# Latent attention core: seeding the score banks of two key tiles with four products on quarters of the array

## The chip, the cores and the metric

The kernel runs on one core of a Trainium2 chip. The metric is the device time of one execution in microseconds (us), as a median over the runs. The engines that matter here are PE (TensorE: matrix products; its weight loads are listed apart as PEld), ACT (ScalarE), DVE (VectorE), POOL (GpSimd) and SP (SyncE, which here only issues transfers).

## The reference, cut to what matters

The program is a decoder of twelve stages over 2048 rows of width 256. One of them is attention of 512 queries per batch over 1536 keys (1024 context rows and the 512 rows themselves), 4 batches, 16 heads of depth 64:

```
q = lat @ Wq
kv_input = jnp.concatenate([x, lat], axis=1)
kv = kv_input @ Wkv
k, v = jnp.split(kv, 2, axis=-1)
dots = jnp.einsum('bhid,bhjd->bhij', q, k) * scale
attn = jax.nn.softmax(dots, axis=-1)
out = jnp.einsum('bhij,bhjd->bhid', attn, v)
```

The softmax subtracts the maximum of every query's row, so the maxima have to be known before the exponentials are taken.

## The kernel before, in words

`latent_core_stage` does this stage's scores, softmax and weighting. It works in 32 groups (4 batches of 8 groups), each a pair of heads; head 0 of the pair lies on rows 0 to 63 of the array and of every operand, head 1 on rows 64 to 127 (`strip(j)`). A group has `nkt` = 12 key tiles of 128 keys. Every product over the depth of 64 therefore comes as two instructions, one per head, on the upper and on the lower half of the array's rows.

Two passes overlap. **Pass A** (`pass_a`, line 1059) forms the scores of a later group in bf16, 128 queries by 512 keys at a time, twelve steps a group; DVE takes the maximum of each (`maxima`, line 1183). After the twelfth, PE turns the maxima (`turn`, line 1066), DVE negates them and splits them in two bf16 parts (`negate`, lines 1192 to 1195, semaphore `row_made`), and SP copies them by DMA into two rows per head of `max_row` (`row`, line 1025, semaphore `row_in`): row 0 and 1 of each half. **Pass B** forms the scores again in f32 with keys on the partitions. `scores(b, g, i)` first writes minus the maxima into the bank of each head with a bf16 product of ones by `max_row` (line 1077, the seed), then adds the f32 product of keys by queries on top (line 1079, two instructions per head). ACT takes the exponential of both banks in one instruction (line 1162, semaphore `exp_done`); POOL and DVE add the weights up (lines 1253 and 1202); `weigh` (line 1089) multiplies the weights by the values, with the two heads side by side in the array's columns; `spread` (line 1099) sums the totals over the keys once a group. The score banks are four: tile `i` uses two of them and tile `i + 1` the other two.

The order is written out by hand. For each pair of tiles PE does: scores of tile i, scores of tile i + 1, a pass A step, (in the fifth pair of a group) the turn, weighing of the two tiles before, (in the second pair) the spread, and a pass A step. Every engine runs the same loop: groups 0 and 1 are written out, a hardware loop of three turns holds groups 2 to 9, 10 to 17 and 18 to 25, and groups 26 to 31 are written out again. The row of maxima of group g + 1 is issued by SP within group g, as soon as `row_made` says so, and PE asks for it (`row_in`) just before the first seed of group g + 1.

```
for i in range(0, nkt, 2):
    scores(b, g, i)
    scores(b, g, i + 1)
```

Of the kernel before, what the change touches and what calls it, by code (L numbers as in the profile page):

```python
# [31 lines left out]
P = 128  # L32
# [6 lines left out]
QUAD = 32  # L39
# [879 lines left out]
def latent_core_stage(k, q_store, k_store, values, nk, scale, att_of):  # L919
# [4 lines left out]
    nc = k.nc  # L924
    HEADS, D, nq = 2, 64, S
    GROUPS = H // HEADS
    nqt, nkt, nwide = nq // P, nk // P, nk // BANK
# [3 lines left out]
    RING, V_RING, TILES = 4, 2, 6  # L931
    A0, B0, ACC, SIDE = 0, 2, 6, 7
    QUARTERS = 4
    QUARTER = nq // QUARTERS
    ROW_PARTS = 2
    assert NP == nkt and nkt % TILES == 0 and nkt % 2 == 0

    def strip(j):
        return slice(j * D, (j + 1) * D)
# [6 lines left out]
    with ExitStack() as held:  # L946
        def sb(what, shape, dt=F32):
            return held.enter_context(nc.sbuf_tensor(f"lc_{what}", shape, dt))

        q_tile = [sb(f"q{r}", [P, nq]) for r in range(RING)]  # L950
        k_tile = [sb(f"k{r}", [P, nk]) for r in range(RING)]
        v_tile = [sb(f"v{r}", [P, nkt, P]) for r in range(V_RING)]
        q_round, k_round = sb("q_round", [P, 2, nq], BF16), sb("k_round", [P, 2, nk], BF16)
        max_row, ones_row = sb("max_row", [P, 2, nq], BF16), sb("ones_row", [P, P], BF16)
# [4 lines left out]
        negative, max_parts = sb("negative", [SLOTS, P]), sb("max_parts", [SLOTS, ROW_PARTS, P], BF16)  # L959
# [8 lines left out]
        def at(b, g, per_group, n):  # L968
            return b * (GROUPS * per_group) + (g * per_group + n)

        def later(b, g, ahead):
            return b + (g + ahead) // GROUPS, (g + ahead) % GROUPS
# [4 lines left out]
        def exists(b, g):  # L977
            return number(b, g) is None or 0 <= number(b, g) < B * GROUPS

        def before(b, g, n):  # L980

            return number(b, g) is not None and number(b, g) < n
# [11 lines left out]
        def pair_at(b, g, i):  # L994

            p = i + AHEAD
            return (*later(b, g, 1 + p // NP), p % NP)

        def loads_done(b, g):
            return 32 * (b * (GROUPS // RING) + g // RING + 1)  # L1000
# [4 lines left out]
        @block.sync  # L1005
        def _(sync):
            k.clear_last_set(sync)

            def load_group(b, g):
                rows = slice(g * P, (g + 1) * P)  # L1010
                sync.dma_start(q_tile[g % RING][:], q_store[rows, bass.ds(b * nq, nq)]).then_inc(loaded[g % RING], 16)
                sync.dma_start(k_tile[g % RING][:], k_store[rows, bass.ds(b * nk, nk)]).then_inc(loaded[g % RING], 16)

            def load_values(b, g):
                sync.dma_start(v_tile[g % V_RING][:], values[bass.ds(b * nkt, nkt), :, g * P:(g + 1) * P].rearrange("i p c -> p i c")
                               ).then_inc(v_loaded[g % V_RING], 16)

            def row(b, g):

                if before(b, g, 1):  # L1020
                    sync.wait_ge(set_up, 1)
                sync.wait_ge(row_made, at(b, g, 1, 1))
                for j in range(HEADS):
                    for p in range(ROW_PARTS):
                        sync.dma_start(max_row[j * D + p:j * D + p + 1, g % 2, :].rearrange("o (i t) -> o i t", t=P),
                                       max_parts[j * nqt:(j + 1) * nqt, p, :]).then_inc(row_in, 16)

            load_group(0, 0)
            load_group(0, 1)
            load_values(0, 0)  # L1030
            load_group(0, 2)
            load_values(0, 1)
            row(0, 0)

            def group(b, g):

                if not before(b, g, 1):
                    sync.wait_ge(pv_done, at(b, g, nkt, 0))
                    if exists(*later(b, g, 1)):
                        load_values(*later(b, g, 1))  # L1040
                if exists(*later(b, g, 3)):
                    load_group(*later(b, g, 3))
                if exists(*later(b, g, 1)):
                    row(*later(b, g, 1))

            for_groups(sync, group)

        @block.tensor
        def _(pe):
# [15 lines left out]
                    pe.wait_ge(inverted, at(b, g, QUARTERS, -QUARTERS))  # L1065
                nc.tensor.transpose(k.ps[0:SLOTS, SIDE, 0:P], row_max[:, g % 2, :], k.ident[:, :]).then_inc(turned, 1)

            def scores(b, g, i):

                if i == 0:  # L1070
                    pe.wait_ge(loaded[g % RING], loads_done(b, g))
                    pe.wait_ge(row_in, 16 * HEADS * ROW_PARTS * at(b, g, 1, 1))
                if not (before(b, g, 1) and i < 2):
                    pe.wait_ge(exp_done, at(b, g, nkt, i - 1))
                out = [k.ps[:, B0 + (i % 2) * HEADS + j, 0:nq] for j in range(HEADS)]
                for j in range(HEADS):
                    nc.tensor.matmul(out[j], ones_row[strip(j), :], max_row[strip(j), g % 2, :], start=True, stop=False)
                for j in range(HEADS):
                    mm = nc.tensor.matmul(out[j], k_tile[g % RING][strip(j), i * P:(i + 1) * P], q_tile[g % RING][strip(j), :], start=False, stop=True)  # L1079
                mm.then_inc(s_ready, 1)  # L1080

            def weigh(b, g, i):
# [27 lines left out]
            def group(b, g):  # L1110
                last, following = later(b, g, -1), later(b, g, 1)
                for i in range(0, nkt, 2):
                    scores(b, g, i)
                    scores(b, g, i + 1)
                    beside_values, beside_scores = pair_at(b, g, i), pair_at(b, g, i + 1)
                    if exists(*beside_values[:2]):
                        pass_a(*beside_values)
                    if i == nkt - AHEAD and exists(*following):
                        turn(*following)
                    if i:  # L1120
                        weigh(b, g, i - 2)
                        weigh(b, g, i - 1)
                    elif exists(*last):
                        weigh(*last, nkt - 2)
                        weigh(*last, nkt - 1)
                    if i == 2 and exists(*last):
                        spread(*last, at(b, g, 1, 1))
                    if exists(*beside_scores[:2]):
                        pass_a(*beside_scores)
# [43 lines left out]
        def _(dve):  # L1173
# [14 lines left out]
            def negate(b, g):  # L1188
                dve.wait_ge(turned, at(b, g, 1, 1))
                if not before(b, g, 1):  # L1190
                    dve.wait_ge(row_in, 16 * HEADS * ROW_PARTS * at(b, g, 1, 0))
                nc.vector.tensor_scalar(max_parts[:, 0, :], k.ps[0:SLOTS, SIDE, 0:P], -1.0, None, ALU.mult).then_inc(high_made, 1)
                nc.vector.tensor_scalar(negative[:, :], k.ps[0:SLOTS, SIDE, 0:P], -1.0, None, ALU.mult).then_inc(high_made, 1)
                dve.wait_ge(high_made, at(b, g, 2, 2))
                nc.vector.tensor_tensor(max_parts[:, 1, :], negative[:, :], max_parts[:, 0, :], ALU.subtract).then_inc(row_made, 1)
# [1591 lines left out]
class ContextFeed:  # L2787
# [5 lines left out]
    RING = 4  # L2793
# [218 lines left out]
```

## Time and profile before

| | us |
|---|---|
| median of 3 runs | 5061.21 |
| fastest and slowest of them | 5048.93 and 5066.54 |
| the profiled execution's own time | 5067.82 |
| its span in the trace | 5066.0 |
| mean granted clock of TensorE | 0.89 |

The span is the time from the first to the last instruction of the profiled execution; 1.8 us lie outside it. The latent core takes some 960 us of it, from about 2842 to 3805 us. Times in the rows below are us from the span's start.

### The profile page before, as it was taken

How to read it: one execution, taken by the hardware profiler on the slowest of the kernel's cores; microseconds unless marked ns; L12 is line 12 of the kernel's file. 1: busy time of each engine (PE TensorE's matmuls, PEld its weight loads, DVE VectorE, ACT ScalarE, POOL GpSimd, SP SyncE). 2: the span in 40 equal slices, each digit the busy share in tenths (PEclk: the TensorE clock that was granted, in tenths of full speed). 3: DMA queues.
4: the chain of work that ended last, by engine and by line, in shares of the span. 5: the costliest groups of instructions: out<-in, count | busy, mean ns of one | idle time of the engine just before them, and what ended most of it. 6: DMA issues, size and time to landing. Idle time of an engine off the chain costs nothing. (4 is left out here: it accounts for less than half of the span.)

```text
span 5066.0 us, 69777 instructions
## 1 busy us (share of the span) xinstructions
PE 4205.1 (83%) x20328; PEld 1984.3 (39%) x20328; DVE 2850.2 (56%) x6426; ACT 2373.5 (47%) x4593; POOL 1482.9 (29%) x1306
## 2 busy tenths in 40 slices
PE   8669766689678997897979799999997988189986
PEld 5322355377443322573234233333335644012223
DVE  3448474501566884104860378778763265298866
ACT  4336431243233775233753355545551255269992
POOL 3111132212130111112120188778880223200111
PEclk9669987799887998898989899999998999579998
DMA  7555212354033332574324321221201044623421
GB/s 250 128 104 116 50 52 34 113 201 150 31 126 56 66 66 64 226 240 136 73 62 158 112 74 59 64 69 59 73 28 45 32 116 83 191 63 89 93 54 37
DMA packets 374291, 486.70 MB, mean 96 GB/s; under 512 B 84772, under 2 KB 288020, under 8 KB 360516
## 3 DMA queue, kind: packets, MB, share of 16 engines
q1 hardware_dynamic: 366528, 447.77, 31.8%
q0 software_dynamic: 6384, 32.61, 2.1%
q8 instruction: 137, 2.24, 0.2%
q10 hardware_dynamic: 1068, 2.66, 0.2%
q14 instruction: 174, 1.43, 0.1%
HBM read 325.07 MB, written 143.92 MB: 93 GB/s over the span
## 5 line engine op out<-in xcount | busy, mean ns | idle before, releaser
L1253 POOL TENSOR_TENSOR lc_totals<-lc_totals,lc_weights 128x1024 f32<-128x1024 f32 (+1 forms) x320 | 623.3, 1948 | 165.0 <-DVE lc_totals L1202 134.4
L1162 ACT ACTIVATE lc_weights<-ps 128x1024 f32<-128x1024 f32 x384 | 393.6, 1025 | 441.3 <-PE ps L1079 431.0
L1183 DVE TENSOR_REDUCE lc_part_max<-ps 128x2 f32<-128x1024 f32 x384 | 466.3, 1214 | 200.2 <-PE ps L1059 198.8
L1079 PE MATMUL ps<-lc_q,lc_k 64*128 64x512 f32 x1536 | 397.0, 595 | 0.0
L1089 PE MATMUL ps<-lc_weights,lc_v 128*64 128x512 f32 x1536 | 372.0, 605 | 0.0
L775 DVE TENSOR_REDUCE l1x_core_part_max<-ps 128x1 f32<-128x512 f32 x512 | 316.5, 681 | 74.8 <-PE ps L599 74.7
L771 DVE CUSTOM_DVE_ANT_0 l3x_core_unused<-ps,l3x_core_mask_q 128x512 f32<-128x512 f32 x512 | 330.8, 686 | 6.7 <-DVE l3x_core_row_max L779 4.9
L734 ACT ACTIVATE l3x_core_weights<-ps 128x512 f32<-128x512 f32 x512 | 327.2, 693 | 8.2 <-PE ps L667 7.9
L734 ACT ACTIVATE l1x_core_weights<-ps 128x512 f32<-128x512 f32 x512 | 266.0, 602 | 83.9 <-PE ps L667 83.8
L717 ACT ACTIVATE ps<-l3x_core_mask_k 128x512 f32<-128x512 f32 x384 | 270.2, 704 | 33.4 <-DMA l3x_core_mask_k<-in_mask_k 33.4
L599 PE MATMUL ps<-l3x_core_k,l3x_core_q 96*128 96x512 bf16 x512 | 215.4, 421 | 53.5 <-DVE l3x_core_part_max L771 38.5
L237 POOL TENSOR_TENSOR proj_parts<-proj_rest,proj_parts 128x512 bf16<-128x512 f32 x112 | 143.5, 1288 | 308.5 <-ACT proj_parts L174 308.2
L599 PE MATMUL ps<-l1x_core_k,l1x_core_q 96*128 96x512 bf16 x512 | 208.9, 411 | 17.2 <-DMA l1x_core_k<-k_parts 13.3
L667 PE MATMUL ps<-l3x_core_q,l3x_core_k 99*128 99x512 bf16 x512 | 199.9, 397 | 18.6 <-ACT ps L717 17.2
L667 PE MATMUL ps<-l1x_core_q,l1x_core_k 99*128 99x512 bf16 x512 | 191.6, 384 | 5.3 <-ACT l1x_core_weights L734 5.3
L1379 DVE SCALAR_TENSOR_TENSOR rn_z<-ps,rn_z 128x256 f32<-128x256 f32 x112 | 45.7, 416 | 261.2 <-PE ps L1350 192.2
L775 DVE TENSOR_REDUCE pyr_core_row_max<-ps 128x1 f32<-128x512 f32 x256 | 158.7, 680 | 54.7 <-PE ps L599 54.5
L1079 PEld LDWEIGHTS ps<-lc_q,lc_k 64*128 64x128 f32 x1536 | 148.3, 189 | 94.0 <-issue 64.9
L775 DVE TENSOR_REDUCE l2a_core_row_max<-ps 128x1 f32<-128x512 f32 x256 | 158.3, 680 | 37.1 <-PE ps L599 37.0
L1059 PE MATMUL ps<-lc_k_round,lc_q_round 64*128 64x512 bf16 x768 | 151.6, 391 | 32.7 <-DVE lc_part_max L1183 21.2
L1089 PEld LDWEIGHTS ps<-lc_weights,lc_v 128*64 128x64 f32 x1536 | 93.3, 136 | 210.3 <-issue 118.8
L734 ACT ACTIVATE pyr_core_weights<-ps 128x512 f32<-128x512 f32 x256 | 134.0, 602 | 79.3 <-PE ps L667 78.9
(479 smaller groups left out, 8594.9 us busy)
## 6 DMA issues: line engine op xcount, KB each, us to landing
cf_w<-in_L1f_w SPq DMA_DIRECT2D x32, 1024.0 KB, 7.3
lc_k<-latent_k SPq DMA_DIRECT2D x32, 768.0 KB, 6.6
lc_v<-latent_values SPq DMA_DIRECT2D x32, 768.0 KB, 4.9
k_parts<-proj_parts SPq DMA_DIRECT2D x56, 384.0 KB, 2.8
latent_k<-feed_staged SPq DMA_DIRECT2D x64, 256.0 KB
latent_values<-feed_staged SPq DMA_DIRECT2D x64, 256.0 KB
q_parts<-proj_parts SPq DMA_DIRECT2D x40, 384.0 KB, 2.9
q_parts<-proj_parts SPq DMA_DIRECT2D x40, 256.0 KB, 3.0
```

What stands on the lines that cost most here:

```text
L599: mm = nc.tensor.matmul(out, q_stack[r][0:rows_a, j, qs], k_stack[r][0:rows_a, j, keys], start=True, stop=not causal)
L667: mm = nc.tensor.matmul(out, k_stack[r][0:rows_b, j, ks], q_stack[r][0:rows_b, j, qs], start=not seeded, stop=not (causal or seeded), skip ...
L717: nc.scalar.activation(k.ps[:, B0 + (g * NS + s) % B_BANKS, 0:nq], seed, ACT.Copy).then_inc(filled, 1)
L734: nc.scalar.activation(weights[:, (g * NS + s) % WEIGHTS, qs], k.ps[:, B0 + (g * NS + s) % B_BANKS, qs], ACT.Exp, scale=scale).then_inc(ex ...
L771: nc.vector.tensor_tensor_reduce(unused[:, n % 2, :], scores, mask_q[:, qi, keys], 1.0, -3.0e38, ALU.add, ALU.max, out).then_inc(a_taken, 1)
L775: nc.vector.reduce_max(out, scores, AX).then_inc(a_taken, 1)
L1059: mm = nc.tensor.matmul(k.ps[:, A0 + j, :], q_round[strip(j), g % 2, qs], k_round[strip(j), g % 2, keys], start=True, stop=True)
L1079: mm = nc.tensor.matmul(out[j], k_tile[g % RING][strip(j), i * P:(i + 1) * P], q_tile[g % RING][strip(j), :], start=False, stop=True)
L1089: mm = nc.tensor.matmul(k.ps[strip(j), ACC, 0:nq], v_tile[g % V_RING][:, i, strip(j)], weights[:, i % TILES, j, :], start=i == 0, stop=i = ...
L1162: nc.scalar.activation(weights[:, i % TILES, :, :], k.ps[:, B0 + (i % 2) * HEADS:B0 + (i % 2 + 1) * HEADS, 0:nq], ACT.Exp, scale=scale).th ...
L1183: nc.vector.reduce_max(own, k.ps[:, A0:A0 + HEADS, :], AX).then_inc(a_taken, 1)
L1253: nc.gpsimd.tensor_tensor(total, total, own, ALU.add).then_inc(added_by_pool, 1)
```

## The change

The seeds of both tiles of a pair are now issued together, ahead of the two score products, by a new function `seed_two`. Each seed is a product over 32 rows instead of 64: tile i uses rows 0 to 31 of each head's half, tile i + 1 rows 32 to 63, so that the four seeds lie on the four quarters of the array's rows (`QUAD` is 32). For this the row of maxima must lie at the start of each quarter; SP issues eight copies of 1 KB a group instead of four. `seed_two` waits for the exponentials of both tiles of the pair before, where each `scores` waited for that of its own banks.

```
                 for j in range(HEADS):
                     for p in range(ROW_PARTS):
-                        sync.dma_start(max_row[j * D + p:j * D + p + 1, g % 2, :].rearrange("o (i t) -> o i t", t=P),
-                                       max_parts[j * nqt:(j + 1) * nqt, p, :]).then_inc(row_in, 16)
+                        for own in (j * D + p, j * D + QUAD + p):
+                            sync.dma_start(max_row[own:own + 1, g % 2, :].rearrange("o (i t) -> o i t", t=P),
+                                           max_parts[j * nqt:(j + 1) * nqt, p, :]).then_inc(row_in, 16)
...
-            def scores(b, g, i):
+            def bank(i, j):
+                return k.ps[:, B0 + (i % 2) * HEADS + j, 0:nq]
+
+            def seed_two(b, g, i):
 
                 if i == 0:
                     pe.wait_ge(loaded[g % RING], loads_done(b, g))
-                    pe.wait_ge(row_in, 16 * HEADS * ROW_PARTS * at(b, g, 1, 1))
+                    pe.wait_ge(row_in, 16 * HEADS * ROW_PARTS * 2 * at(b, g, 1, 1))
                 if not (before(b, g, 1) and i < 2):
-                    pe.wait_ge(exp_done, at(b, g, nkt, i - 1))
-                out = [k.ps[:, B0 + (i % 2) * HEADS + j, 0:nq] for j in range(HEADS)]
+                    pe.wait_ge(exp_done, at(b, g, nkt, i))
+                for n in range(2):
+                    for j in range(HEADS):
+                        own = slice(j * D + n * QUAD, j * D + (n + 1) * QUAD)
+                        nc.tensor.matmul(bank(i + n, j), ones_row[own, :], max_row[own, g % 2, :], start=True, stop=False,
+                                         tile_position=(j * D + n * QUAD, 0))
+
+            def scores(b, g, i):
+
                 for j in range(HEADS):
-                    nc.tensor.matmul(out[j], ones_row[strip(j), :], max_row[strip(j), g % 2, :], start=True, stop=False)
-                for j in range(HEADS):
-                    mm = nc.tensor.matmul(out[j], k_tile[g % RING][strip(j), i * P:(i + 1) * P], q_tile[g % RING][strip(j), :], start=False, stop=True)
+                    mm = nc.tensor.matmul(bank(i, j), k_tile[g % RING][strip(j), i * P:(i + 1) * P], q_tile[g % RING][strip(j), :], start=False, stop=True)
                 mm.then_inc(s_ready, 1)
...
                 for i in range(0, nkt, 2):
+                    seed_two(b, g, i)
                     scores(b, g, i)
                     scores(b, g, i + 1)
```

On PE, one pair of tiles in the middle of a group reads as follows before (line 1059 is pass A, 1077 the seeds, 1079 the f32 scores, 1089 the weighing; the f32 products stand once here and are two instructions each in the profile).

```order
L1059 MATMUL ps<-lc_k_round,lc_q_round 128x512 x2
L1077 MATMUL ps<-lc_max_row,lc_ones_row 128x512 x2
L1079 MATMUL ps<-lc_q,lc_k 128x512 x2
L1077 MATMUL ps<-lc_max_row,lc_ones_row 128x512 x2
L1079 MATMUL ps<-lc_q,lc_k 128x512 x2
L1059 MATMUL ps<-lc_k_round,lc_q_round 128x512 x2
L1089 MATMUL ps<-lc_weights,lc_v 64x512 x4
```

The same pair of the changed kernel, where the lines are 1060, 1082, 1088 and 1098:

```order
L1060 MATMUL ps<-lc_k_round,lc_q_round 128x512 x2
L1082 MATMUL ps<-lc_max_row,lc_ones_row 128x512 x4
L1088 MATMUL ps<-lc_q,lc_k 128x512 x4
L1060 MATMUL ps<-lc_k_round,lc_q_round 128x512 x2
L1098 MATMUL ps<-lc_weights,lc_v 64x512 x4
```

The second pair of seeds moved ahead of the first scores; the four seeds stand between pass A and the scores, both of which use halves of the rows.

On SP, the transfers around one group's row of maxima (its queries, its keys, the row, then the next group's values) before:

```order
L1011 DMA lc_q<-latent_q 128x512
L1012 DMA lc_k<-latent_k 128x1536
L1025 DMA lc_max_row<-lc_max_parts 1x4x128 x4
L1015 DMA lc_v<-latent_values 128x12x128
L1011 DMA lc_q<-latent_q 128x512
```

and in the changed kernel:

```order
L1011 DMA lc_q<-latent_q 128x512
L1012 DMA lc_k<-latent_k 128x1536
L1026 DMA lc_max_row<-lc_max_parts 1x4x128 x8
L1015 DMA lc_v<-latent_values 128x12x128
L1011 DMA lc_q<-latent_q 128x512
```

Nothing changed places on SP; the row's issues are twice as many.

## Rows read from the trace of the kernel before

**Rows 1.** The page: busy time of the engines.

```profile
PE 4205.1 (83%) x20328; PEld 1984.3 (39%) x20328; DVE 2850.2 (56%) x6426; ACT 2373.5 (47%) x4593; POOL 1482.9 (29%) x1306
```

**Rows 2.** Windows, one stretch of the stage: PE, PEld, DVE, ACT, POOL busy, clock.

```profile
3400.00:3600.00 200.00, 196.86 (x1025) 68.03 (x1027) 159.48 (x165) 101.45 (x103) 157.60 (x82) 0.99 0.20 66
```

**Rows 3.** Groups by line within 2880 to 3790 us: busy, mean ns | idle before.

```profile
L1183 DVE TENSOR_REDUCE lc_part_max<-ps 128x2 f32<-128x1024 f32 x369 | 447.9, 1214 | 182.8 <-PE ps L1059 181.3
L1162 ACT ACTIVATE lc_weights<-ps 128x1024 f32<-128x1024 f32 x380 | 389.5, 1025 | 437.2 <-PE ps L1079 427.0
```

**Rows 4.** Timeline of PE, first pair of group 8: start, duration, line, count.

```profile
3107.24 0.39 PE L1059 MATMUL ps<-lc_k_round,lc_q_round 64*128 64x512 bf16 x2
3107.47 0.39 PE L1077 MATMUL ps<-lc_max_row,lc_ones_row 64*128 64x512 bf16 x2
3107.70 1.03 PE L1079 MATMUL ps<-lc_q,lc_k 64*128 64x512 f32 x4
3108.55 0.38 PE L1077 MATMUL ps<-lc_max_row,lc_ones_row 64*128 64x512 bf16 x2
3108.77 1.03 PE L1079 MATMUL ps<-lc_q,lc_k 64*128 64x512 f32 x4
3109.63 0.38 PE L1059 MATMUL ps<-lc_k_round,lc_q_round 64*128 64x512 bf16 x2
3109.94 1.94 PE L1089 MATMUL ps<-lc_weights,lc_v 128*64 128x512 f32 x8
3111.81 0.39 PE L1059 MATMUL ps<-lc_k_round,lc_q_round 64*128 64x512 bf16 x2
```

**Rows 5.** Timeline of PE at the turn of the maxima.

```profile
3128.70 0.38 PE L1059 MATMUL ps<-lc_k_round,lc_q_round 64*128 64x512 bf16 x2
3129.01 0.27 PE L1066 MATMUL ps<-ident,lc_row_max 128*8 128x128 f32 x1
```

**Rows 6.** Timeline, all engines, from the maxima's last part to SP's next work.

```profile
3102.37 0.70 DVE L1195 TENSOR_TENSOR lc_max_parts<-lc_negative,lc_max_parts 8x128 bf16<-8x128 f32 x1
...
3103.10 2.46 SPq L1025 DMA_DIRECT2D lc_max_row<-lc_max_parts  x4
...
3107.47 0.10 PEld L1077 LDWEIGHTS ps<-lc_max_row,lc_ones_row 64*128 64x128 bf16 x2
...
3112.08 0.39 SPq L1015 DMA_DIRECT2D lc_v<-latent_values  x1
```

**Rows 7.** The row's issues; transfer rate over 3103 to 3107 us; a similar transfer's landing.

```profile
L1025 SPq DMA_DIRECT2D lc_max_row<-lc_max_parts x128: 572/573/684, 2874.5 to 3772.1; - x128
...
GB/s 0 0 0 0 0 0 0 0 0 0 0 0 0 10 0 0 0 0 0 8 3 0 0 0 0 5 5 0 0 0 0 3 8 0 0 0 0 0 0 0
...
l3a_core_q<-l3a_core_max_parts SPq DMA_DIRECT2D x48, 4.0 KB, 1.9
```

**Rows 8.** The seeds' weight loads: min/median/max ns, first and last start.

```profile
L1077 PEld LDWEIGHTS ps<-lc_max_row,lc_ones_row x768: 92/94/148, 2879.6 to 3795.9; 64*128 64x128 bf16 x192
```

**Rows 9.** Timeline: two exponentials, and the seed of the next pair.

```profile
3118.74 2.10 ACT L1162 ACTIVATE lc_weights<-ps 128x1024 f32<-128x1024 f32 x2 [3.31 <-PE ps L1079]
...
3122.00 0.38 PE L1077 MATMUL ps<-lc_max_row,lc_ones_row 64*128 64x512 bf16 x2
```

**Rows 10.** Timeline of PE at the hardware loop's jump back.

```profile
3168.22 0.61 PE L1077 MATMUL ps<-lc_max_row,lc_ones_row 64*128 64x512 bf16 x2 [3.80 <-issue]
```

**Rows 11.** PE in other cores: products, idle times; windows give PE busy and clock.

```profile
533.90 1.07 PE L634 MATMUL ps<-pyr_core_weights,pyr_core_v 128*32 128x512 f32 x8
536.92 0.39 PE L667 MATMUL ps<-pyr_core_q,pyr_core_k 99*128 99x512 bf16 x1 [1.95 <-DMA pyr_core_q<-pyr_core_max_parts]
...
538.60:542.00 3.40, 3.40 (x14) 0.77 (x13) 2.19 (x6) 1.82 (x4) 0.19 (x1) 0.50 0.00 1
...
4232.83 0.39 PE L667 MATMUL ps<-l3a_core_q,l3a_core_k 102*128 102x512 bf16 x1 [1.42 <-DMA l3a_core_q<-l3a_core_max_parts]
...
4236.00:4240.00 4.00, 4.00 (x40) 1.88 (x38) 2.80 (x8) 2.94 (x8) 3.92 (x6) 1.00 0.86 189
```

More of the change, by code:

```diff
@@ L1190, in negate @@
                 if not before(b, g, 1):
-                    dve.wait_ge(row_in, 16 * HEADS * ROW_PARTS * at(b, g, 1, 0))
+                    dve.wait_ge(row_in, 16 * HEADS * ROW_PARTS * 2 * at(b, g, 1, 0))
                 nc.vector.tensor_scalar(max_parts[:, 0, :], k.ps[0:SLOTS, SIDE, 0:P], -1.0, None, ALU.mult).then_inc(high_made, 1)
```

## The prediction, made before the changed kernel ran

> **What bounds the kernel now.** I read the page first. The profiled execution took 5067.8 us, its span 5066.0; PE is busy for 83% of it [rows 1]. The change touches one stage of about 960 us, so I asked for windows inside that stage. In 200 us of its middle PE is busy for 196.9 us at a granted clock of 0.99, which is the 2.4 GHz level; DVE has 159 us, POOL 158, ACT 101 [rows 2]. The groups by line say the same: ACT idles 437 us before its exponentials, nearly all of it for PE's scores, and DVE idles 183 us before its maxima, for PE's pass A [rows 3]. PE bounds the stage. A nanosecond more or less on PE, between two of its instructions or in them, goes to the end, 192 times over if it is there once a pair of tiles (32 groups of 6 pairs). A wait of PE once a group counts up to 32 times. The row transfers start at 2874.5 and 3772.1 us, 31 groups apart [rows 7], so a group takes 29.0 us on average.
>
> Next I read PE's timeline over one pair, by its starts, since the durations of pipelined products overlap [rows 4]. The two products of a head pair start together and run side by side. A bf16 pair followed by work on the same halves takes 0.22 us (3108.55 to 3108.77); four f32 instructions take 0.86 (3108.77 to 3109.63), 0.43 per side-by-side pair. Where the array's division changes there is more: pass A, followed by the weighing, takes 0.31 instead of 0.22, so 0.09 extra; the weighing, eight instructions, takes 1.87 (3109.94 to 3111.81) instead of 4 x 0.43 = 1.72, so 0.15 extra, for its entry's second f32 weight load and for its exit. A round trip from halves of the rows to halves of the columns and back costs 0.24 us. Does it also cost that when only the rows' division changes? One place bears on it: pass A before the turn of the maxima, which uses all 128 rows and 8 columns, again takes 0.31 us (3128.70 to 3129.01) [rows 5].
>
> Last I followed the row of maxima [rows 6]. DVE ends the last part at 3103.07 (3102.37 + 0.70). SP issues four copies back to back, 3103.10 to 3105.56. PE loads the seeds' ones at 3107.47, 0.23 after pass A started [rows 4], an ordinary step: the row was already there. One issue takes 0.573 us [rows 7], so the four start (2.46 - 0.57) / 3 = 0.63 apart and the fourth starts at 3104.98. The rate of transfers, in slices of 0.1 us, shows four bursts, the last ending near 3106.3 [rows 7]: 1.3 us after its issue. When the semaphore follows isn't in a row of these copies; a similar transfer of 4 KB lands 1.9 us after its issue [rows 7]. I take 1.6, with 1.3 and 1.9 as bounds, so the row is there by about 3106.6, 0.9 us early.
>
> **The change part by part.**
>
> *The seeds' time.* Four seeds side by side take the time of two: one step of 0.22 us goes in each pair, -0.22 x 192 = -42 us. That four products on quarters run at once is nowhere in this trace for rows. For columns it is: eight f32 instructions on quarters of the columns show 1.07 us in all [rows 11], where four on halves show 1.03 [rows 4]. I take full overlap; the other end is none, 0 us.
>
> The Trainium skill, "TensorE: Matmul & The Clock Gate", section "Measured speedup vs the span model", gives 3.07 times for four row tiles of 512 columns, not 4. An estimate from that page: the four seeds would take 0.22 x 4 / 3.07 = 0.29 us instead of 0.22, and the sum would be 13 us higher. No run here shows it yet.
>
> *Two more changes of division in each pair.* Before, pass A, seeds and scores all use halves of the rows. Now the array goes to quarters for the seeds and back to halves. Entry to bf16 seeds: 0.09 as before the weighing, and 0.01 since the seeds' weight load can't be hidden any more, 0.10. Exit to f32 scores: the weighing's 0.15 is its exit to bf16, 0.10, and 0.05 for its second f32 weight load; a change into f32 thus costs 0.09 + 0.05, and I add 0.02 as the scores' f32 weights have 128 columns where the weighing's have 64: 0.16. Together 0.26 x 192 = +50 us. The low bound is 0.09 twice, +35; the high one doubles the weight-load part of the exit, 0.31 x 192 = +60. If only the rows' division were free it would be 0; the row at the turn speaks against that, though it is an f32 product through all rows.
>
> The Trainium skill, "TensorEngine Tiling (Array Packing)", section "Tiling Modes", says that changing the tiling mode, not just the tile, drains the engine. By that rule rows behave as columns do, and the -42 us are about given back; the trace agrees where columns change, with 0.09 us, and probably where rows alone do.
>
> *Two more instructions side by side* start 0.01 us apart at most: +1 us.
>
> Seeds, divisions and issue come to -42 + 50 + 1 = +9 us (from -6 to +19).
>
> *The row of maxima.* SP now issues eight copies. The eighth starts 7 x 0.63 = 4.4 us after the first, at 3107.5 in the group shown, and lands 1.6 later, at 3109.1. PE asks at 3107.47, plus some 0.04 from the pair between: it waits 1.6 us (1.3 to 1.9). Behind that instruction stands all of PE's queue: scores, pass A, weighing; so ACT, DVE and POOL idle too and nothing is caught up, as PE is the bound on both sides. DVE's part before the copies isn't sped up, so the wait comes back in each group. In groups 10 and 18 it is hidden: there PE jumps back in the loop and idles 3.80 us just before its first seed [rows 10]. Group 0 is apart: its row starts at 2874.5 [rows 7] and PE loads the seeds at 2879.6 [rows 8]; the eighth copy lands at 2874.5 + 4.5 + 1.6 = 2880.6, +1 us. That leaves 29 groups: 29 x 1.6 = +46, and 1 more, +47 us (+38 to +56).
>
> *What costs nothing.* The seeds now wait for both exponentials of the pair before. ACT ends the second at 3120.84 and PE seeds at 3122.00 [rows 9], 1.16 us of cover; the first scores come 0.26 us later, by the two changes of division, so about 0.9 remains. Without that cover each pair would lose what is missing. SP's own next work, the next values, starts at 3112.08, and its issues of the row ended at 3105.56 [rows 6]; four more take 2.5 us of those 6.5. POOL's queue isn't passed.
>
> **The sum:** +9 + 47 = +56 us on the profiled 5067.8, 5124. Against the median of the runs, 5061.2, which lies 6.6 us below the profiled execution, that is 5117 us, 1.1% slower. Own range, from the bounds: -6 + 38 = +32 to +19 + 56 = +75, 5093 to 5136.
>
> **The rivals.**
>
> *The clock falls in the new wait.* In another core PE idled 1.95 us, and from 538.6 to 542.0 us the clock was 0.50 (1.2 GHz); after an idle time of 1.42 us it stayed at 1.00 [rows 11]. The new 1.6 us lie between. 3.4 us at half speed lose 1.7 us; in all 29 groups +49, so 5117 to 5166. For it: nearness to 1.95. Against: this stage is denser on both sides than either place. 0.18.
>
> *Going between halves and quarters of the rows costs nothing.* Then seeds and issue give -41. But PE comes to the next group 0.22 us earlier and waits 1.8 instead of 1.6: 29 x 1.8 + 1 = +53. Sum +12, 5073, inside what can't be told from no change, or just above. For it: no row has two bf16 products between halves and quarters. Against: [rows 5]. 0.12.
>
> *The row isn't late* (the other side). If eight copies are issued closer than 0.63 us, or land sooner, the wait goes; PE asks 4.4 us after the first issue (3107.51 less 3103.10), so the wait is gone when they start less than (4.4 - 1.6) / 7 = 0.40 us apart. Then only +9 remains, 5070, not slower by what can be told; with free divisions too it would be -41, 5020. Against: 128 issues have a minimum of 572 ns [rows 7]. 0.05 for the first, 0.03 for both.
>
> *The seeds don't run four at once*, so that the change doesn't do what it says: by twos, with the divisions' cost, +42 on the forecast, 5159. In between, as after the page's figure, 5130. 0.07.
>
> My forecast has the remaining 0.55.
>
> **How the numbers follow.** A measurement of this kernel can tell about 0.3%, 15 us, from no change: 5046 to 5076. Faster needs both free divisions and a row in time: 0.03, and 0.01 for what I don't see. No change: the row in time (0.05) and half of the free divisions (0.06), less a little: 0.10. Slower has the rest, 0.86. The range takes in the free divisions at its low end and most of the clock's and of the overlap's case at its high end: 5074 to 5160.
>
> **What the changed profile would show.** The four seeds starting within 0.02 us and pass A to seeds 0.31 to 0.32 us apart; seeds to scores about 0.38; the first scores' f32 of a pair followed by the second's after 0.86. Eight issues of 0.57 us in 5.0 us. PE idle 1.6 us before the first seeds of 29 groups, released by the DMA, and a group of 30.6 to 30.9 us. The granted clock at 0.99 in the middle windows; 0.9 or less means the first rival. A step of 0.22 from pass A to the seeds means free divisions; seeds that start in twos 0.2 us apart mean the last rival. The prediction is wrong on its main term if PE's wait before the first seed is under 0.5 us or over 3.

## The result, and the profile after

The changed kernel takes 5145.08 us (median of 4 runs, 5139.41 to 5147.14), the kernel before 5061.49 us (4 runs, the same chip): ratio 1.0168, 95% interval 1.0153 to 1.0182. That is 84 us slower, where 56 were forecast. The direction held, and so did the stated range, 5074 to 5160 us. The narrower range that came from the bounds of the terms alone, 5093 to 5136, did not: a third of the loss was in no term of the sum.

The page of the changed kernel, busy time of the engines; it stands against [rows 1].

```profile
span 5145.5 us, 69905 instructions
PE 4230.8 (82%) x20328; PEld 1963.5 (38%) x20328; DVE 2889.0 (56%) x6426; ACT 2351.4 (46%) x4593; POOL 1467.0 (29%) x1306
```

The window 3400 to 3600 us, columns as in [rows 2]: PE is busy 186 of 200 us instead of 197, at the same granted clock, 0.99 (the 2.4 GHz level). The new waits did not bring the clock down.

```profile
3400.00:3600.00 200.00, 186.34 (x945) 58.41 (x943) 153.60 (x155) 90.41 (x96) 144.90 (x77) 0.99 0.18 57
```

The seeds' own rows give the length of the stage, from the first seed's weight load to the last's: 2878.6 to 3880.2 is 1001.6 us. Before it was 2879.6 to 3795.9, 916.3 us [rows 8]. The difference of 85.3 us is about the whole loss, 83.6 by the medians, so the rest of the program can be left out. This length comes from one profiled execution each, and still it is a sharper measure than the total: the kernel before and the three variants that should equal it (e5, e8 and e11 below) lie between 914.3 and 916.8 us, while the runs of the kernel before alone are spread over 17 us. The two rows are the weight loads and the issues of the row of maxima, 256 of the same 0.573 us as in [rows 7].

```profile
L1082 PEld LDWEIGHTS ps<-lc_max_row,lc_ones_row x768: 90/91/101, 2878.6 to 3880.2; 32*128 32x128 bf16 x192
...
L1026 SPq DMA_DIRECT2D lc_max_row<-lc_max_parts x256: 572/573/681, 2872.4 to 3855.6; - x128
```

PE's timeline over an ordinary pair answers to [rows 4]: start, duration, line.

```profile
3142.26 0.39 PE L1060 MATMUL ps<-lc_k_round,lc_q_round 64*128 64x512 bf16 x2
3142.58 0.39 PE L1082 MATMUL ps<-lc_max_row,lc_ones_row 32*128 32x512 bf16 x4
3142.91 1.99 PE L1088 MATMUL ps<-lc_q,lc_k 64*128 64x512 f32 x8
3144.73 0.38 PE L1060 MATMUL ps<-lc_k_round,lc_q_round 64*128 64x512 bf16 x2
3145.04 1.94 PE L1098 MATMUL ps<-lc_weights,lc_v 128*64 128x512 f32 x8
3146.91 0.39 PE L1060 MATMUL ps<-lc_k_round,lc_q_round 64*128 64x512 bf16 x2
```

Four seeds are shown with 0.39 us, as two were. Pass A to the seeds takes 0.32 us, the seeds to the scores 0.33, and the eight f32 instructions 1.82 where 4 x 0.43 = 1.72 would do. The pair is 3146.91 - 3142.26 = 4.65 us long; the pair of [rows 4] was 3111.81 - 3107.24 = 4.57, and the others before without a turn or a spread take 4.55, from seeds to seeds. The weight loads of the f32 scores show where the 0.10 lies, here in the first pair of group 8: after the first four, which come together, the next two start 0.54 us later and the last two 0.43 after those.

```profile
3131.78 0.30 PEld L1088 LDWEIGHTS ps<-lc_q,lc_k 64*128 64x128 f32 x4 [0.23 <-issue]
3132.32 0.19 PEld L1088 LDWEIGHTS ps<-lc_q,lc_k 64*128 64x128 f32 x2 [0.24 <-issue]
3132.75 0.19 PEld L1088 LDWEIGHTS ps<-lc_q,lc_k 64*128 64x128 f32 x2 [0.23 <-issue]
```

Around the first seeds of group 8, all engines, to be read against [rows 6] (the turn of the maxima comes first):

```profile
3123.08 0.27 PE L1067 MATMUL ps<-ident,lc_row_max 128*8 128x128 f32 x1
...
3124.83 0.59 DVE L1205 TENSOR_TENSOR lc_max_parts<-lc_negative,lc_max_parts 8x128 bf16<-8x128 f32 x1
...
3125.45 4.92 SPq L1026 DMA_DIRECT2D lc_max_row<-lc_max_parts  x8
...
3129.80 0.39 PE L1060 MATMUL ps<-lc_k_round,lc_q_round 64*128 64x512 bf16 x2
...
3131.46 0.40 PE L1082 MATMUL ps<-lc_max_row,lc_ones_row 32*128 32x512 bf16 x4 [1.27 <-DMA lc_max_row<-lc_max_parts]
...
3134.03 1.23 DVE L1193 TENSOR_REDUCE lc_part_max<-ps 128x2 f32<-128x1024 f32 x1 [2.57 <-PE ps L1060]
...
3135.13 2.34 POOL L1258 TENSOR_TENSOR lc_totals<-lc_weights 128x1024 f32<-128x1024 f32 x1 [0.49 <-ACT lc_weights L1172]
3135.17 2.85 DVE L1212 TENSOR_TENSOR lc_totals<-lc_totals,lc_weights 128x512 f32<-128x512 f32 x1
...
3137.94 1.21 DVE L1193 TENSOR_REDUCE lc_part_max<-ps 128x2 f32<-128x1024 f32 x1
...
3139.21 0.39 PE L1060 MATMUL ps<-lc_k_round,lc_q_round 64*128 64x512 bf16 x2 [0.79 <-DVE lc_part_max L1193]
```

The maxima are made at 3125.42, the last of eight issues ends at 3130.37 (3125.45 + 4.92), and PE's seeds start at 3131.46, where pass A had started at 3129.80: 1.66 us instead of 0.32. This wait was forecast. The second was not. Eight microseconds after those seeds PE stands again, for a pass A step whose bank DVE has not read. DVE was late since its addition of the last tile's weights took 2.85 us: it began 0.04 us after an addition of POOL's of 2.34 us and ended 0.55 us after that one. In the kernel before, the same addition stood at 3111.19, beside the last of three additions of POOL's, and took 1.66 us; the maxima behind it ended at 3113.99, 0.20 us before pass A came for the bank:

```profile
3106.06 6.25 POOL L1253 TENSOR_TENSOR lc_totals<-lc_totals,lc_weights 128x1024 f32<-128x1024 f32 x3 [0.62 <-DVE lc_totals L1202]
3112.26 2.80 POOL L1248 TENSOR_TENSOR lc_totals<-lc_weights 128x1024 f32<-128x1024 f32 x1
...
3111.19 1.66 DVE L1202 TENSOR_TENSOR lc_totals<-lc_totals,lc_weights 128x512 f32<-128x512 f32 x1
3112.78 1.21 DVE L1183 TENSOR_REDUCE lc_part_max<-ps 128x2 f32<-128x1024 f32 x1
...
3114.19 0.38 PE L1059 MATMUL ps<-lc_k_round,lc_q_round 64*128 64x512 bf16 x2
```

Group 8 is no exception: additions of DVE's of more than 2.5 us occur 30 times in the stage of the changed kernel and twice in the kernel before. The waits of the whole stage (who, for what, total us, times, longest) show both waits of PE:

```profile
PE ps L1082 <- DMA lc_max_row<-lc_max_parts: 28.1, 22, 1.4
PE ps L1060 <- DVE lc_part_max L1193: 22.0, 30, 1.3
PE ps L1082 <- issue: 17.5, 9, 3.5
```

The row's wait is spread over two of these lines. Seven of the nine waits put down to "issue" are the row's too, by their place and length; the other two, 3.5 us each, stand at the jumps of the loop, where the forecast had the wait hidden. That makes 22 + 7 = 29 waits, as forecast.

### The profile page after: what moved, and what is told of

Same layout as the page of the kernel before. It is cut to its first block and busy times, and to the rows that moved or that the text cites. A ratio compares the mean times of both kernels' runs of the same rounds, so it can differ in the third digit from the quotient of the medians.

```text
span 5145.5 us, 69905 instructions
## 1 busy us (share of the span) xinstructions
PE 4230.8 (82%) x20328; PEld 1963.5 (38%) x20328; DVE 2889.0 (56%) x6426; ACT 2351.4 (46%) x4593; POOL 1467.0 (29%) x1306
## 5 line engine op out<-in xcount | busy, mean ns | idle before, releaser
L1172 ACT ACTIVATE lc_weights<-ps 128x1024 f32<-128x1024 f32 x384 | 372.8, 1021 | 550.6 <-PE ps L1088 550.6
L1212 DVE TENSOR_TENSOR lc_totals<-lc_totals,lc_weights 128x512 f32<-128x512 f32 x128 | 179.3, 1401 | 25.9 <-POOL lc_totals L1263 20.2
L1088 PEld LDWEIGHTS ps<-lc_q,lc_k 64*128 64x128 f32 x1536 | 134.3, 189 | 137.3 <-issue 137.3
```

What stands on the lines that cost most here:

```text
L1088: mm = nc.tensor.matmul(bank(i, j), k_tile[g % RING][strip(j), i * P:(i + 1) * P], q_tile[g % RING][strip(j), :], start=False, stop=True)
L1172: nc.scalar.activation(weights[:, i % TILES, :, :], k.ps[:, B0 + (i % 2) * HEADS:B0 + (i % 2 + 1) * HEADS, 0:nq], ACT.Exp, scale=scale).th ...
L1212: nc.vector.tensor_tensor(own, own, weights[:, i % TILES, 1, :], ALU.add).then_inc(added_by_vector, 1)
```

## The experiments

Eleven kernels ran, in three lots, each lot on one chip beside the kernel before. "Stage" is the length from the first to the last seed weight load of the profiled execution, as above; before it is 916.3 us. Differences of 2 or 3 us in it mean nothing, by the four kernels named there. The medians, each against its own lot's kernel before, agree with it within 7 us.

| kernel | median, us | ratio (95% interval) | stage, us | against before |
|---|---|---|---|---|
| changed | 5145.1 | 1.0168 (1.0153 to 1.0182) | 1001.6 | +85.3 |
| e1, eight copies, old seeds | 5134.8 | 1.0149 (1.0134 to 1.0165) | 992.3 | +76.0 |
| e2, changed, four copies | 5078.9 | 1.0039 (1.0025 to 1.0052) | 930.5 | +14.2 |
| e3, changed, DVE's addition moved | 5116.6 | 1.0118 (1.0103 to 1.0134) | 971.5 | +55.2 |
| e4, both | 5077.8 | 1.0034 (1.0022 to 1.0046) | 929.5 | +13.2 |
| e5, new order, seeds on halves | 5058.2 | 0.9995 (0.9986 to 1.0003) | 915.5 | -0.8 |
| e6, new order, two quarters only | 5114.1 | 1.0112 (1.0097 to 1.0126) | 970.1 | +53.8 |
| e7, old order, quarters | 5181.9 | 1.0240 (1.0227 to 1.0253) | 1043.8 | +127.5 |
| e8, before, DVE's addition moved | 5057.4 | 0.9994 (0.9986 to 1.0003) | 914.3 | -2.0 |
| e9, e2 with six issues | 5074.4 | 1.0031 (1.0019 to 1.0043) | 930.8 | +14.5 |
| e10, seeds behind the weighing | 5045.1 | 0.9974 (0.9964 to 0.9985) | 906.5 | -9.8 |
| e11, the same place, halves | 5060.7 | 1.0010 (1.0002 to 1.0019) | 916.8 | +0.5 |

My theory after reading the two traces had three terms: the late row, a knock-on of its wait through DVE, and the changes of division less the saved step. The main rival laid the second wait to the new order of seeds and scores.

**e1: the copies alone.** The kernel before, with twice the copies; the extra ones go to a buffer that nothing reads, and the first seeds wait for all eight (that edit isn't shown).

```
-                        sync.dma_start(max_row[j * D + p:j * D + p + 1, g % 2, :].rearrange("o (i t) -> o i t", t=P),
-                                       max_parts[j * nqt:(j + 1) * nqt, p, :]).then_inc(row_in, 16)
+                        for copy in (max_row, spare_row):
+                            sync.dma_start(copy[j * D + p:j * D + p + 1, g % 2, :].rearrange("o (i t) -> o i t", t=P),
+                                           max_parts[j * nqt:(j + 1) * nqt, p, :]).then_inc(row_in, 16)
```

> The kernel before, with the row of maxima copied eight times a group instead of four; the four new copies go to a spare buffer that nothing reads, and the first seed of a group waits for all eight. Seeds as before, on halves. Theory (three terms: the late row, a knock-on of that wait on DVE, and the changes of the array's division): no change of division here, so PE waits about 1.6 us before the first seed of 29 groups (the eighth copy at 5.98 after the maxima are made, PE ready at 4.39), +47 us, and the knock-on follows the wait, up to 0.96 us a group, +28: 5110 to 5136, likeliest 5134. Rival A (the pass A wait of 0.96 us comes from the new order of seeds and scores, not from the late row): 5109, and no PE wait for DVE in the group's second pair. Rival B (the row's lateness is not the copies' number): no more than 5066.

Measured 5134.8 us. Both waits are there with the old seeds in the old order, so the order isn't the cause of the second:

```profile
3128.87 0.39 PE L1079 MATMUL ps<-lc_max_row,lc_ones_row 64*128 64x512 bf16 x2 [1.54 <-DMA lc_spare_row<-lc_max_parts]
...
3132.49 2.36 POOL L1250 TENSOR_TENSOR lc_totals<-lc_weights 128x1024 f32<-128x1024 f32 x1 [0.52 <-ACT lc_weights L1164]
3132.59 2.81 DVE L1204 TENSOR_TENSOR lc_totals<-lc_totals,lc_weights 128x512 f32<-128x512 f32 x1
...
3136.59 0.39 PE L1061 MATMUL ps<-lc_k_round,lc_q_round 64*128 64x512 bf16 x2 [0.84 <-DVE lc_part_max L1185]
```

The late copies cost 76 us here, somewhat more than in the changed kernel (71, as e2 shows): PE comes to the first seeds 4.41 us after the maxima are made where the changed kernel would come 4.70 after, so it waits 1.65 us instead of 1.34. The granted clock stays at 0.98 in the window of [rows 2] even so.

**e2: the same rows in four transfers.** Each transfer writes one row of both heads, 64 rows apart, so that all eight rows arrive by four issues (the counts that are waited for change with it).

```
-                for j in range(HEADS):
-                    for p in range(ROW_PARTS):
-                        for own in (j * D + p, j * D + QUAD + p):
-                            sync.dma_start(max_row[own:own + 1, g % 2, :].rearrange("o (i t) -> o i t", t=P),
-                                           max_parts[j * nqt:(j + 1) * nqt, p, :]).then_inc(row_in, 16)
+                for p in range(ROW_PARTS):
+                    for own in (p, QUAD + p):
+                        sync.dma_start(max_row[own:own + D + 1:D, g % 2, :].rearrange("j (i t) -> j i t", t=P),
+                                       max_parts[:, p, :]).then_inc(row_in, 16)
```

> The changed kernel with the same eight rows copied by four transfers a group, each to one row of both heads. Theory: the row lands 3.5 to 3.6 us after the maxima are made, as before, so the wait before the first seed and its knock-on on DVE both go; what stays is 0.09 to 0.10 us a pair for two changes of division less the saved step, 192 times, +19 us: 5080. Rival A (the wait of pass A comes from the new order): 5100 to 5108, with PE waiting for DVE 0.7 to 1 us in a group's second pair. Rival C (a transfer of two rows takes longer to issue or land than one of one row, so part of the wait stays): 5085 to 5120.

Measured 5078.9, as expected. An issue is even a little shorter, 0.51 us, and no wait for the row is left among PE's waits; the last row below has the pass A wait at 2.9 us where it was 22.0.

```profile
L1025 SPq DMA_DIRECT2D lc_max_row<-lc_max_parts x128: 495/510/604, 2868.4 to 3781.3; - x128
...
PE ps L1059 <- DVE lc_part_max L1192: 2.9, 3, 1.3
```

**e3, e4 and e8: the collision.** DVE adds the last tile's weights after the second maxima of the new group instead of before; in e3 in the changed kernel, in e4 on top of e2, in e8 in the kernel before.

```
-                    if i == 0 and exists(*last) and on_vector(nkt - 1):
+                    if i == 1 and exists(*last) and on_vector(nkt - 1):
                         add_weights(*last, nkt - 1)
```

> The changed kernel, eight copies, but DVE adds the last tile's weights of a group one step later, behind the second maxima of the next group instead of ahead of them. Theory: the wait before the first seed stays at 1.3 us, but POOL's first addition of the new group no longer holds DVE's just ahead of the maxima that pass A waits for; the 0.8 to 1 us in the second pair go: 5145 - 25 = 5120. Rival D (the collision only moves, and the next pass A or the spread waits instead): 5140 to 5148.

> Both: four transfers of two rows, and DVE's addition moved. Theory: with the row in time the knock-on is already gone, so that the move adds nothing: as e2, 5080. If DVE's addition also costs PE something without the wait, up to 10 us less.

> The kernel before with DVE's addition of the last tile's weights moved one step later as in e3. Theory: nothing waits for it there, so 5061 within 5 us. If it frees pass A now and then: down to 5050.

Measured 5116.6, 5077.8 and 5057.4. In e3 PE still waits for the row, but DVE's addition now starts when POOL's is nearly done and takes 0.68 us instead of 2.85:

```profile
3148.70 0.39 PE L1082 MATMUL ps<-lc_max_row,lc_ones_row 32*128 32x512 bf16 x4 [1.26 <-DMA lc_max_row<-lc_max_parts]
...
3152.27 2.35 POOL L1258 TENSOR_TENSOR lc_totals<-lc_weights 128x1024 f32<-128x1024 f32 x1 [0.37 <-ACT lc_weights L1172]
...
3154.60 0.68 DVE L1212 TENSOR_TENSOR lc_totals<-lc_totals,lc_weights 128x512 f32<-128x512 f32 x1
3155.50 0.38 PE L1060 MATMUL ps<-lc_k_round,lc_q_round 64*128 64x512 bf16 x2
```

The move takes 30 us off the changed kernel's stage, 1 us off e2's and 2 off that of the kernel before. So these 30 us are the knock-on of the late row. The move takes DVE's addition out of the way of the second maxima and shortens it at once; that the length alone would do is worked out from the rows: with 0.68 us in the old place the second maxima of group 8 would end near 3137.5, and pass A could not start before 3138.3 anyway. What stays of e3 over e2, 971.5 - 930.5 = 41 us, is the row's wait itself.

**e5, e6 and e7: division and overlap apart.** e5 has the changed kernel's order with the seeds of both tiles on halves; e6 gives both tiles' seeds the first quarter of each head's half, so that they run two at a time; e7 is the old order with each seed on 32 rows. All three use the four copies of the kernel before.

```
# e5, in seed_two
+ nc.tensor.matmul(bank(i + n, j), ones_row[strip(j), :], max_row[strip(j), g % 2, :], start=True, stop=False)
# e6, in seed_two
- own = slice(j * D + n * QUAD, j * D + (n + 1) * QUAD)
+ own = slice(j * D, j * D + QUAD)
# e7, in scores of the kernel before
- nc.tensor.matmul(out[j], ones_row[strip(j), :], max_row[strip(j), g % 2, :], start=True, stop=False)
+ own = slice(j * D, j * D + QUAD)
+ nc.tensor.matmul(out[j], ones_row[own, :], max_row[own, g % 2, :], start=True, stop=False, tile_position=(j * D, 0))
```

> The changed kernel's order (all seeds of a pair ahead of both score products, one wait for both exponentials) but seeds on halves of the rows as before and four copies. No change of division, no fourfold overlap. Theory: the order costs nothing, the seeds take two steps of 0.22 us: 5061 within 5 us. Rival A (the order makes pass A wait for DVE): 5080 to 5090.

> The changed kernel's order with seeds over 32 rows, but both tiles' seeds on the first quarter of each head's half, so that only two can run side by side; four copies. It has the two changes of division a pair and not the saved step. Theory: two changes cost 0.30 to 0.31 us a pair as the changed kernel's steps show (0.32 in, 0.32 and a first f32 step longer by 0.10 out, against 0.22 each): +59 us, 5120, and starts of the second seeds 0.22 after the first. Rival (changes of the rows' division are cheap and it is the fourfold overlap that is short): under 5085.

> The kernel before, in its old order, with each tile's seeds over 32 rows of each head's half instead of 64; four copies. Four changes of division a pair instead of none. Theory: 4 changes cost 0.6 us a pair, +115 us: 5176, perhaps less by what DVE's waits give back. Rival (a change costs only when the step that follows has an f32 weight load to hide, so that entries are free): +60 to +75, 5125 to 5135.

Measured 5058.2, 5114.1 and 5181.9. e5 shows that the order, and the one wait for both exponentials, cost nothing. e6 less e5 is the price of two changes of the rows' division a pair with nothing saved: 54.6 us of the stage, 0.28 a pair. (In an ordinary pair it is 0.31, 4.86 us from seeds to seeds against 4.55; some of it is hidden, as at the jumps of the loop, where PE idles 3.0 and 3.1 us before the seeds instead of 3.8.) e6 less e2 is what the fourfold overlap saves: 39.6 us, 0.21 a pair. e6's timeline shows the missing overlap, 0.53 us from seeds to scores where the changed kernel has 0.33:

```profile
3136.26 0.60 PE L1081 MATMUL ps<-lc_max_row,lc_ones_row 32*128 32x512 bf16 x4
3136.79 0.70 PE L1087 MATMUL ps<-lc_q,lc_k 64*128 64x512 f32 x2
```

e6 is 6 us below what I had put down. e7 is 6 us above, but hardly since the changes cost more: an ordinary pair takes 5.17 us, so that four changes cost 0.62. Its timeline has all four at full price: 0.33 and 0.31 into and out of the first seeds, 1.06 instead of 0.86 for the scores up to the next ones, 0.32 out.

```profile
3129.06 0.39 PE L1059 MATMUL ps<-lc_k_round,lc_q_round 64*128 64x512 bf16 x2
3129.39 0.39 PE L1078 MATMUL ps<-lc_max_row,lc_ones_row 32*128 32x512 bf16 x2
3129.70 1.13 PE L1080 MATMUL ps<-lc_q,lc_k 64*128 64x512 f32 x4
3130.76 0.39 PE L1078 MATMUL ps<-lc_max_row,lc_ones_row 32*128 32x512 bf16 x2
3131.08 1.13 PE L1080 MATMUL ps<-lc_q,lc_k 64*128 64x512 f32 x4
```

The rest is the collision once more. In 30 groups of e7 DVE's addition takes more than 2.5 us, and PE waits for the maxima in the group's second pair, which is 0.3 us longer than the changes make it. The row comes in time here, so the collision needs no stall of PE: a schedule that is shifted in another way can make it too. e6 has three such additions, e2 three.

```profile
3144.05 2.34 POOL L1249 TENSOR_TENSOR lc_totals<-lc_weights 128x1024 f32<-128x1024 f32 x1 [0.59 <-ACT lc_weights L1163]
3144.14 2.79 DVE L1203 TENSOR_TENSOR lc_totals<-lc_totals,lc_weights 128x512 f32<-128x512 f32 x1
...
3148.13 0.39 PE L1059 MATMUL ps<-lc_k_round,lc_q_round 64*128 64x512 bf16 x2 [0.22 <-DVE lc_part_max L1184]
```

**e9: how much lateness is free.** e2 with two more copies to a spare buffer, six issues, all waited for.

```
+                    sync.dma_start(spare_row[p:p + D + 1:D, g % 2, :].rearrange("j (i t) -> j i t", t=P),
+                                   max_parts[:, p, :]).then_inc(row_in, 16)
```

> e2 with two more copies a group into a spare buffer, six issues, all waited for. Theory: the sixth copy lands 0.02 + 5 x 0.63 + 1.6 = 4.8 us after the maxima are made; PE gets to the first seed at about 4.7, so the wait is 0.1 us or so a group and its knock-on on DVE is at most as long: as e2 plus 0 to 6 us, 5079 to 5085. Rival (each issue costs PE in proportion, whatever its slack): e2 plus half of the 66 us between e2 and the changed kernel, 5112.

Measured 5074.4, and a stage of 930.8 us against e2's 930.5. (The two ran on different chips, so their stages compare better than their medians.) The median is 5 us below what I had put down, since not even the 0.1 us a group came: PE's products wait 1.0 us for the spare copies in the whole stage. Two issues more cost nothing: the wait is a threshold, not a price per issue.

**e10 and e11: another place.** The seeds of the next pair are issued behind the weighing, ahead of a bf16 pass A step. The very first seeds stand ahead of the first group (not shown). e11 has them there on halves, with the four copies of the kernel before.

```
                 for i in range(0, nkt, 2):
-                    seed_two(b, g, i)
                     scores(b, g, i)
...
                         spread(*last, at(b, g, 1, 1))
+                    if i + 2 < nkt:
+                        seed_two(b, g, i + 2)
+                    elif exists(*following):
+                        seed_two(*following, 0)
                     if exists(*beside_scores[:2]):
                         pass_a(*beside_scores)
```

> e2 with the four seeds moved: issued right behind the weighing of the pair before (and the spread), ahead of the pass A step that stood there. The array goes from halves of the columns to quarters of the rows, where it went to halves of the rows, and then to the bf16 pass A instead of the f32 scores. One change of division more than in the kernel before instead of two, and none into f32. Theory: one change into bf16 costs 0.10 us, the saved step gives 0.22: -0.12 x 192 = -22 us against the kernel before, 5038. The row is needed 0.3 us earlier and has 0.9. Rival E (the exponentials aren't done by then, or pass A's shift makes DVE late): 5060 or more. Rival F (from columns to rows a change to quarters costs more than one to halves): 5050 to 5060.

> The seeds at the place of e10, but on halves of the rows and with the four copies of the kernel before: the place alone. Theory: the place costs nothing and gives nothing, 5061 within 5 us, 20 us above e10. Rival (the place itself is what helps): as e10.

Measured 5045.1 and 5060.7. e10 is the one version faster than both kernels: 12 us by the medians, 0.26%, clear of the interval, and 9.8 in the stage. Its ordinary pair takes 3134.61 - 3130.16 = 4.45 us against 4.55, and 0.12 less was expected. Once a group, in the fifth pair, a pass A step waits for DVE's maxima. That pair is 3139.60 - 3134.61 = 4.99 us long, where 4.45 and the 0.20 of the turn make 4.65. The row, which is now asked for earlier, holds PE only twice, by 0.6 us in all; one of the two is the last line here.

```profile
3130.16 0.39 PE L1081 MATMUL ps<-lc_max_row,lc_ones_row 32*128 32x512 bf16 x4
3130.49 0.39 PE L1059 MATMUL ps<-lc_k_round,lc_q_round 64*128 64x512 bf16 x2
3130.72 1.88 PE L1087 MATMUL ps<-lc_q,lc_k 64*128 64x512 f32 x8
...
3134.61 0.40 PE L1081 MATMUL ps<-lc_max_row,lc_ones_row 32*128 32x512 bf16 x4
...
3137.21 0.39 PE L1059 MATMUL ps<-lc_k_round,lc_q_round 64*128 64x512 bf16 x2 [0.16 <-DVE lc_part_max L1196]
...
3139.60 0.39 PE L1081 MATMUL ps<-lc_max_row,lc_ones_row 32*128 32x512 bf16 x4
...
3144.35 0.40 PE L1081 MATMUL ps<-lc_max_row,lc_ones_row 32*128 32x512 bf16 x4 [0.24 <-DMA lc_max_row<-lc_max_parts]
```

Of the expected 22 us, 10 to 12 came. The missing part has the size of the pass A wait, 0.34 us a group or 11 in all; this was read from the trace, not tried. e11 shows that the place by itself gives nothing.

## Why the prediction was right, and where it wasn't

*The saved step.* Forecast -42 us with full overlap; e6 less e2 gives -39.6 (33 by the medians, whose intervals are too wide to decide). Full overlap is right: from seeds to scores, four seeds on quarters take 0.33 us, two take 0.31 or 0.32 (e7), and two after two 0.53 (e6). The Trainium skill, "TensorE: Matmul & The Clock Gate", section "Measured speedup vs the span model", has 3.07 times for four row tiles, by which the step would have saved less; the runs do not agree with it here.

*The changes of division.* Forecast +50 us, from the column changes' rows and the turn; e6 less e5 gives +54.6. By the sizes in the timeline the entry is 0.10 as forecast, the exit 0.21 instead of 0.16: 0.11 between seeds and scores and 0.10 in the f32 steps behind. That this 0.10 is the second weight load of 128 columns, which isn't hidden, fits the rows of the weight loads but wasn't tried. The Trainium skill, "TensorEngine Tiling (Array Packing)", section "Tiling Modes", says that a change of mode drains the engine; these rows agree in that each change costs 0.10 us or so, also where the rows alone change. Together with the step, +9 was forecast and e2 shows +14.2; the term was low by 5.

*The late row.* Forecast +47 us (1.6 a group), measured +41 (e3 less e2); a group's wait is 1.66 - 0.32 = 1.34 us. The mechanism and the count of issues and of groups were right, and so was the landing: from the maxima to the seeds it is 3131.46 - 3125.42 = 6.04 us, and the forecast's numbers give 6.03. The size was off as PE would come to the first seed 3129.80 + 0.32 - 3125.42 = 4.70 us after the maxima, as it does in e2, and I had 4.44. Of these 0.26 us, 0.09 is the entry to the quarters between pass A and these very seeds, which I had priced for every pair and left out here; 0.05 is the pair between, longer by 0.09 and not by 0.04; and 0.12 is that the maxima are made 2.34 us after the turn (3123.08 to 3125.42) instead of 2.46 (3100.61 to 3103.07 before), as DVE's last part takes 0.59 us instead of 0.70.

*The step that failed* is "so ACT, DVE and POOL idle too and nothing is caught up, as PE is the bound on both sides". It took a wait of PE for its own length and no more. In fact the other engines don't resume in the order in which they stood. Before, DVE's addition of tile 11 overlapped the end of a POOL addition and took 1.66 us, with 0.20 to spare. After the wait, the exponential of the new group's second tile and the group's first maxima end close together, POOL's addition and DVE's start within 0.04 us of each other, DVE's takes 2.85 us, the second maxima are late, and pass A stands. That is 30 us (e3), and by itself more than the 28 us by which the forecast fell short. The sign that would have told it was on the list: a group was to take 30.6 to 30.9 us, and it takes 31.2 (from the first seeds of group 8, at 3131.5, to those of group 9, at 3162.7).

The terms as measured are +14 + 41 + 30 = +85, the stage's own +85.3. As differences of one kernel to the next they must add up to it; what supports them is where they lie. Measured from seeds to seeds, the changed kernel is longer than e2 by 41 us in the last pairs of the groups, which end at the next group's first seeds, by 27 in the second pairs, by 3 in the first, and by nothing in the other three.

*Luck.* The forecast was right in direction for its main reason. That the time fell into the range was in part luck: the range was stretched to 5160 for a slower clock and for seeds that overlap less, and neither happened. What happened instead, the knock-on, stood in no bound of any term.

*The cover of the exponentials* held: e5 is even with the kernel before. *SP's own work* stayed clear of the longer issue, which ends at 3130.37 with the next transfer at 3136.05. *The clock* did not fall: 0.99 in the window above, 0.891 over the whole span against 0.89. The rival with the clock is out at waits of 1.3 us, and of 1.65 by e1; what 1.9 would do here is not shown.

## What to carry to other kernels

In this kernel a change of how the array is divided costs 0.1 us, and 0.2 into f32; two of them cost more than the 0.22 us of one 512-column bf16 step. Put such a product where the array changes its division anyway and where bf16 follows, and count the changes before counting the products saved. Small transfers queued on one engine cost their issue one after the other; see how late the last may land, and write two rows with one transfer when the rows are a fixed step apart. A stall of the bounding engine, or any other shift, does more than move the schedule: look for pairs of instructions on DVE and POOL that will now start together. Here such a pair cost 30 us on top of the stall's 41.

## What the runs showed of the hardware

Two additions with operands in SBUF, one on DVE and one on POOL, do not share time when they begin together: DVE's took 0.68 us alone and 2.85 when it started 0.04 us after POOL's of 2.34, and it ended 0.55 us after that one. POOL's kept its 2.34. The other way round POOL waits: in the kernel before, its addition that began at 3112.26, while DVE's was running until 3112.85, took 2.80. The Trainium skill, "Trainium Architecture — The Big Picture", section "What this means for kernel authors", calls the port pair of the two an exclusive lock, not a split; these rows agree.

A transfer of two rows of 1 KB to destinations 64 partitions apart took 0.51 us to issue, one of a single row 0.57.

Four bf16 products on quarters of the rows, each into a bank of its own, ran fully side by side: 0.33 us to the next step, where two on quarters of the rows take 0.31 or 0.32 and two after two 0.53.
